# Layer 1 of a two-layer graph attention kernel: rows multiplied by ScalarE and summed by one operation a batch, V halves made a chunk ahead, groups of four tiles closed by pairs

## The reference, cut to what matters

```python
# x: (8192, 256), adj: (8192, 8192) int32, symmetric, about 8 neighbours a row and itself
h = maximum(layernorm(x), 0)                       # layer 0
x = x + leaky_relu(softmax(where(adj == 0, -1e9, e_left[:, None] + e_right[None, :])) @ (h @ W), 0.2)
h = maximum(layernorm(x), 0)                       # layer 1
h1 = h @ a[:256];  h2 = h @ a[256:]
e = leaky_relu(h1 + h2.T, 0.01)
x = x + softmax(where(adj > 0, e, -9e15), axis=1) @ h
```

## Time and profile before

| | us |
|---|---|
| times of three executions | 1916.23, 1925.32, 1924.2 |
| median | 1924.2 |
| the profiled execution's own time | 1914.35 |
| its span | 1912.5 |
| PE, busy | 1691.5 (88%) |
| DVE, busy | 1203.0 (63%) |
| ACT, busy | 973.4 (51%) |
| POOL, busy | 651.6 (34%) |

### The profile page before, as it was taken

The page is one execution under the profiler, slowest core; times in us unless marked ns, Lnnn a source line. Parts: engine busy times, 40 slices in busy tenths (PEclk is TensorE's granted clock), DMA queues, the critical chain, the costliest instruction groups (busy, mean ns, idle before and its releaser), DMA issues. The chain is left out here.

```text
span 1912.5 us, 37724 instructions
## 1 busy us (share of the span) xinstructions
PE 1691.5 (88%) x13955; PEld 1391.3 (73%) x13955; DVE 1203.0 (63%) x4595; ACT 973.4 (51%) x1367; POOL 651.6 (34%) x607
## 2 busy tenths in 40 slices
PE   6888999999999999999999397677888888978878
PEld 5646888888888888888888285454666667757657
DVE  7488888988888888674444377652435445435434
ACT  5987665665666556666662375432333233323322
POOL 0000000000000000026665548755656657665562
PEclk9998999999999999999999698877889889979889
DMA  8529998888988889989994534533333333433331
GB/s 287 182 76 386 342 349 325 314 311 321 354 320 326 318 310 331 355 333 378 386 379 104 130 94 134 160 80 88 101 89 83 111 89 94 117 100 99 88 92 52
DMA packets 142801, 410.60 MB, mean 215 GB/s; under 512 B 26193, under 2 KB 90066, under 8 KB 109906
## 3 DMA queue, kind: packets, MB, share of 16 engines
q1 hardware_dynamic: 108434, 329.85, 47.6%
q0 software_dynamic: 27904, 73.43, 13.9%
q10 hardware_dynamic: 6336, 5.77, 1.0%
HBM read 368.94 MB, written 40.03 MB: 214 GB/s over the span
## 5 line engine op out<-in xcount | busy, mean ns | idle before, releaser
L984 PE MATMUL banks<-HV,adjT 128*128 128x257 f16 x8192 | 938.8, 274 | 16.7 <-DVE adjT L658 8.8
L984 PEld LDWEIGHTS banks<-HV,adjT 128*128 128x128 fp8e4 x8192 | 792.5, 98 | 148.2 <-DVE HV L688 23.7
L1639 PE MATMUL banks<-Vp,adjp 128*128 128x257 f16 x2560 | 540.6, 292 | 115.4 <-issue 59.2
L1639 PE MATMUL banks<-Vn,adjn 128*128 128x257 f16 x2560 | 538.1, 291 | 48.9 <-issue 47.7
L1264 POOL DMA_INDIRECT gat<-h_of_layer,rec x420 | 465.8, 1109 | 275.5 <-issue 117.9
L444 ACT ACTIVATE adj_f<-adj_i 128x2048 fp8e4<-128x2048 int32 x256 | 480.1, 1898 | 6.6 <-DMA adj_i<-in_adj 6.5
L1300 ACT ACTIVATE adjn<-h1bc,nh 128x512 fp8e5<-128x512 f32 x320 | 212.1, 716 | 446.2 <-remote 272.1
L1639 PEld LDWEIGHTS banks<-Vp,adjp 128*128 128x128 fp8e4 x2560 | 261.2, 103 | 192.3 <-issue 126.5
L1639 PEld LDWEIGHTS banks<-Vn,adjn 128*128 128x128 fp8e4 x2560 | 262.2, 103 | 124.8 <-issue 76.5
L425 POOL DMA_DIRECT2D HV<-x_after_layer x44 | 25.5, 580 | 773.4 <-DVE rank L911 741.3
L1473 DVE TENSOR_TENSOR adjn<-adjp,adjn 128x1024 uint16<-128x1024 uint16 x80 | 55.4, 692 | 334.8 <-ACT adjn L1300 296.0
(11 more groups left out here) (158 smaller groups left out, 1395.2 us busy)
## 6 DMA issues: line engine op xcount, KB each, us to landing
adj_i<-in_adj SPq DMA_DIRECT2D x256, 1024.0 KB
h_of_layer<-hh SPq DMA_DIRECT2D x64, 129.0 KB
hs<-h_of_layer SPq DMA_DIRECT2D x64, 129.0 KB
xt<-in_x SPq DMA_DIRECT2D x64, 128.0 KB
packed_adj<-pk SPq DMA_DIRECT2D x64, 128.0 KB
x_after_layer<-x SPq DMA_DIRECT2D x64, 128.0 KB
HV<-in_x SPq DMA_DIRECT2D x14, 512.0 KB, 8.8
gat<-h_of_layer,rec POOLq DMA_INDIRECT x420
```

The source lines that it names most:

```text
L984: last = nc.tensor.matmul(acc[b][:, 0:DV], adjT_h[:, b, i, q, :, h], V0[:, jb, s, 0:DV], start=(jb == 0 and s == 0), stop=(jb == T - 1 and ...
L1639: mm = nc.tensor.matmul(bank[2 * i + part][:, 0:DV], m[:, i * P:(i + 1) * P], V[:, j, s, 0:DV], start=(j == 0 and s == 0), stop=(j == T - ...
```

## The change

It has four parts, all in layer 1.

1. **Rows.** ACT multiplies each gathered row by its weight in place (`scale_rows`, one instruction a row), and DVE adds up a batch by one reduction (`sum_rows`). The sum of a batch that isn't a tile's last is written behind the rows of the next batch's buffer, which has a seventh place for it, and is summed with them. Join and second accumulator are gone.
2. **When.** The weights of a batch are made in the turn of its chunk n, the larger is taken and the rows are multiplied in turn n+1, and they are summed in turn n+2. A table `taken(n)` gives the batches of chunk n: it begins with chunk 0 and holds 94 rows by the end of group 0; batches 86 and 87 (9 rows) are done behind the last chunk.
3. **V halves.** `high_chunk` and `low_chunk` make the halves a chunk or two ahead: chunk 0 ahead of everything, and then those of chunk n+2 on ACT and of chunk n+1 on DVE in turn n. `unpack` also stands one turn earlier.
4. **Closing.** In the last chunk of a group and in the first of the next one PE goes through the tiles by pairs: all four `jb` for tiles 0 and 1, and then for tiles 2 and 3. `take_sums` and `scale_sums` come in two halves, the first of which waits for the new semaphore `closed`.

```diff
-        FIRST = 1.35
-        HEAD = 3.0
+        FIRST = 1.13
+        HEAD = -2.0
+        TAIL = 1.4
...
-            gat = sb("gat", [P, NBUF, BS, ROW], f32)
-            sacc = sb("sacc", [P, 2, 2, DV], f32)
+            gat = sb("gat", [P, NBUF, BS + 1, ROW], f32)
+            sacc = sb("sacc", [P, 2, DV], f32)
...
-                        pool.wait_ge(row_added, begin[k - NBUF + 1])
+                        pool.wait_ge(summed, k - NBUF + 1)
...
+                def scale_rows(k):
+                    m, s0, s1 = batch[k]
+                    if s0 == 0:
+                        load_rows(m)
+                    act.wait_ge(w8_ready, k + 1)
+                    for i in range(s1 - s0):
+                        x = gat[:, k % NBUF, i, 0:DV]
+                        made = nc.scalar.activation(x, x, ACT.Copy, scale=w8[:, k % 2, i:i + 1])
+                    made.then_inc(scaled, 1)
...
+                high_chunk(0)
                 act.wait_ge(nh2_ready, 1)
                 act.wait_ge(h1bc_in[0], 16)
-                act.wait_ge(hb_ready, 2)
                 for h in range(2):
                     signs(h, 0, 0, 0, h, False)
+                high_chunk(1)
+                act.wait_ge(hb_ready, 2)
                 for n in range(C):
...
                     if g > 0 and c == 0:
-                        scale_sums(g - 1, g == 1)
+                        for half in range(2):
+                            scale_sums(g - 1, half, g == 1)
                     if n + 1 < C:
...
                             signs(2 * n + 2 + h, n + 1, g1 % 2, c1, h, 2 * n + 2 + h >= RB)
+                    for k in taken(n - 1):
+                        scale_rows(k)
+                    if n + 2 < NC:
+                        high_chunk(n + 2)
+                    for k in taken(n):
+                        weights(k)
+                for k in taken(C - 1):
+                    scale_rows(k)
+                for half in range(2):
+                    scale_sums(NGD - 1, half, NGD == 1)
+                for k in range(weighed[C], len(batch)):
+                    weights(k)
+                    scale_rows(k)
...
+                def sum_rows(k):
+                    m, s0, s1 = batch[k]
+                    b = s1 - s0
+                    dve.wait_ge(scaled, k + 1)
+                    if s0:
+                        dve.wait_ge(summed, k)
+                    if k == last[m]:
+                        if m >= 2:
+                            dve.wait_ge(so_ready, m - 1)
+                        to = sacc[:, m % 2, :]
+                    else:
+                        to = gat[:, (k + 1) % NBUF, batch[k + 1][2] - batch[k + 1][1], 0:DV]
+                    nc.vector.reduce_sum(to, gat[:, k % NBUF, 0:b + (1 if s0 else 0), 0:DV]
+                                         .rearrange("p s c -> p c s"), AX.X).then_inc(summed, 1)
...
+                unpack(0, 0, 0, False)
+                low_chunk(0)
                 dve.wait_ge(ab_ready, 1)
+                closing = []
                 for n in range(C):
                     g, c = n // NC, n % NC
                     negatives(n, g, c)
                     positives(n, c)
                     if g > 0 and c == 0:
-                        take_sums(g - 1)
+                        take_sums(g - 1, 0)
+                        take_sums(g - 1, 1)
+                    for m in closing:
+                        divide(m)
+                    if n + 1 < NC:
+                        low_chunk(n + 1)
+                    for m in closing:
+                        add_x1(m)
+                    closing = []
+                    for k in taken(n - 2):
+                        sum_rows(k)
+                        closing += [m for m in range(NS) if last[m] == k]
+                    if n + 1 < C and (n + 1) % UB == 0:
+                        unpack(n + 1, (n + 1) // NC, (n + 1) % NC, n + 1 >= 2 * UB)
                     if g > 0 and c == 1:
                         add_negatives(g - 1)
+                    for k in taken(n - 1):
+                        larger(k)
...
                 def group(g, first):
                     for c in range(NC):
                         n = g * NC + c
                         pe.wait_ge(pos_ready, n + 1)
                         pe.sem_inc(masks_seen, 1)
+                        halved = c == NC - 1 or (c == 0 and not first)
+                        for half in range(2 if halved else 1):
+                            some = range(half * G // 2, half * G // 2 + G // 2) if halved else range(G)
+                            for jb in range(CB):
+                                add_tile(g, c, jb, some, first)
```

More of the change, by code:

```diff
@@ L1047, in two_layer_graph_attention @@
                 batch.append((m, slots[m] * i // parts, slots[m] * (i + 1) // parts))
-        row = [(m, s, k) for k, (m, s0, s1) in enumerate(batch) for s in range(s0, s1)]
-        begin = [row.index((m, s0, k)) for k, (m, s0, s1) in enumerate(batch)]
         at = [sum(slots[:m]) for m in range(NS + 1)]
@@ L1053, in two_layer_graph_attention, with taken @@
         pace = [max(0.0, FIRST * min(n, NC) + max(0, n - NC) - HEAD) for n in range(C)]
-        rows_by = [len(row) * a / pace[-1] for a in pace]
-        rows_by = [0] + [int(a + 1e-6) for a in rows_by]
-        def lead_of(q):
-            return sum(1 for b in begin if b < q + LEAD) if q < len(row) else len(batch)
-        def ended(q):
-            if q == len(row):
-                return NS
-            return sum(1 for m in range(NS - 1) if q > at[m + 1] + min(4, slots[m + 1] - 1))
-        def awaited(q):
-            return max(0, sum(1 for m in range(NS) if at[m] < q) - 2)
+        rows_in = [at[NS] * a / (pace[-1] + TAIL) for a in pace]
+        weighed = [0] + [sum(1 for m, s0, s1 in batch if at[m] + s1 <= a) for a in rows_in]
+        def taken(n):
+            return range(weighed[n], weighed[n + 1]) if n >= 0 else range(0)
         ctx = ExitStack()
@@ L1372, in dense @@
                             if c == 0 and tail:
-                                scale_sums(g - 1, False)
+                                for half in range(2):
+                                    scale_sums(g - 1, half, False)
                     even = NGD + 1 + (NGD + 1) % 2
@@ L1380, in _ @@
                             dense(k * 2 + b, b, k * 16 + 16, True)
-                    scale_sums(NG - 1, False)
+                    for half in range(2):
+                        scale_sums(NG - 1, half, False)
             @block.vector
@@ L1592, in _ @@
-                add_negatives(NGD - 1)
+                    for k in taken(n - 1):
+                        larger(k)
+                for m in closing:
+                    divide(m)
+                    add_x1(m)
+                for k in taken(C - 2):
+                    sum_rows(k)
+                    for m in range(NS):
+                        if last[m] == k:
+                            divide(m)
+                            add_x1(m)
+                for k in taken(C - 1):
+                    larger(k)
+                    sum_rows(k)
+                    for m in range(NS):
+                        if last[m] == k:
+                            divide(m)
+                            add_x1(m)
@@ L1593, in _ @@
+                take_sums(NGD - 1, 0)
+                take_sums(NGD - 1, 1)
+                add_negatives(NGD - 1)
+                for k in range(weighed[C], len(batch)):
+                    larger(k)
+                    sum_rows(k)
+                    for m in range(NS):
+                        if last[m] == k:
+                            divide(m)
+                            add_x1(m)
                 with dve.If(dve.value_load(redi[0:1, 0:1]) > 0):
@@ L1608, in _ @@
                         dense(g, True)
-                    take_sums(NG - 1)
+                    take_sums(NG - 1, 0)
+                    take_sums(NG - 1, 1)
                     add_negatives(NG - 1)
@@ L1615, in _, with add_tile @@
                 nc.tensor.transpose(bank[7][0:T, 0:P], h1all[:, :], idf[:, :]).then_inc(h1T_ps, 1)
+                add_last = [None]
+                def add_tile(g, c, jb, some, first):
+                    j = c * CB + jb
+                    if first:
+                        pe.wait_ge(v_ready, 2 * j + 2)
+                    masks = (adjp_h[:, c // UB % 2, (c % UB * CB + jb) // 2, :, jb % 2],
+                             adjn_h[:, c % 2, jb // 2, :, jb % 2])
+                    for i in some:
+                        for part, (m, V) in enumerate(zip(masks, (Vp, Vn))):
+                            if j == 0:
+                                if first and i == 0 and part == 0:
+                                    pe.wait_ge(h1T_sb, 1)
+                                if not first:
+                                    pe.wait_ge(evn_ready if part else pos_taken,
+                                               g * G - G + i + 1)
+                                    pe.sem_inc(masks_seen, 1)
```

(5 more changed lines are left out.)

151 lines of the change are left out of this document (40 added, 111 removed).

## The result

The changed kernel takes 1993.2 us (median of four, 1978.1 to 2016.8) against 1924.8 of the kernel before; the ratio is 1.033 with a 95% interval of 1.027 to 1.039. The forecast was 1880 and a range up to 1930. The profiled execution took 1978.1, its span is 1976.2. Ratios leave out executions in a slow state of the chip, here that of 2016.8 us and further down one of 4294 us (r7), which is why 1.033 is not 1993.2 / 1924.8.

What follows compares the result with a forecast made beforehand. The prediction took PE to bound the kernel, with 254 us lost to waits and slow issue. Its terms gave 1914.4 - 19 - 18 - 10 - 6 + 13 = 1874, plus 6 for the profiled execution: 1880 us, range 1825 to 1930.

Steps and rivals of the forecast that it cites:

- What bounds the kernel: Layer 1: PE bounds; 21 stretches of slow issue, 120 us in excess, each starting 9 us or more into a POOL run.
- The other 96.5 us I leave: Groups 1 to 4: PE's remaining stalls stay as they are, 96.5 us, since POOL's work a turn is the same.
- the -18 for group 1: Group 1: its stall of 23.5 us goes, so the group takes 153 us instead of 171.
- Rows on ACT: Later turns: ACT's rows (2.0 us) and DVE's batch sums (2.7 us each) stay hidden under PE's 7.1 us.
- the slower rival: DVE's batch sums: the stride costs far more, 16 ns per output, 4.2 us a batch and more; 1938 us at 5.6; chance 0.13.
- the cheap rival: DVE's batch sums: the reduction costs 1.2 ns an element whatever the stride, giving 1856 us; chance 0.12.
- Group 0: Group 0: a chain of 10.5 us a turn, ending at 1252 against 1271, a gain of 19 us.
- Closing by pairs: Group closings: PE's waits of 14.1 us shrink, -10 us, and half the slow clock behind them goes, -6 us.
- The end: Behind the last chunk: batches 86 and 87 stand behind ACT's last sums, 28.8 us against 15.9, +13 us.
- Buffers held too long: Gather buffers: freed two turns after the gather, so PE goes at POOL's pace in parts, +45 us, 1925 us; chance 0.17.
- Stalls vanish: Groups 1 to 4: no POOL run reaches 9 us, most of the 96.5 us goes, about 1800 us; chance 0.13.

Runs made afterwards that it cites:

- r7: A follow-up run that the text does not identify further; one execution of 4294 us, in a slow state of the chip, was left out of its ratio.
- e1: Changed kernel, with POOL waiting behind each batch of gathers until the batch has landed: 1891.8 us, ratio 0.985 to the kernel before.
- e2: Kernel before, with only POOL's wait behind each batch of gathers added: 1936.3 us, ratio 1.009.
- b2: Changed kernel with a 128x1536 memset on POOL behind each batch, in a session with slow issue: 1824.8 us against 1911.3, ratio 0.951.
- c1: Changed kernel with the unpacking back at the head of its turn, in a quiet session: 1735.8 us against 1753.6 of the kernel before, ratio 0.990.
- e3: Kernel before with the closing by pairs alone: 1914.9 us, ratio 0.999.
- e4: Changed kernel with five gather buffers instead of four: 1965.2 us, ratio 1.024 to the kernel before.
- a1: Changed kernel itself, timed again in a later session beside the kernel before: 1969.0 us against 1920.9, ratio 1.024.
- r8: Changed kernel with a 128x1536 memset on POOL behind each batch, in a quiet session: 1819.2 us, ratio 1.037 to the kernel before.

## Why the prediction was wrong, by its steps

**What bounds the kernel.** Right: PE, and the 21 stretches belong to POOL's runs. e1, e2 and b2 show what was only read there. One reading was off: slow issue begins from 8.2 us into a run on, as in the run of the earlier trace rows at 1388.9, and not at 9 or more.

**The step that failed** is "The other 96.5 us I leave, as POOL's work a turn (5 x 1.37) is the same", with the -18 for group 1 beside it. POOL's work was the same, and slow issue went from 121 to 183 us. I had priced the stalls by POOL's amount of work. The runs show that they hang on gathers that follow one another without a break (e1, e2, b2), and that the new order pays more for a microsecond of such a run (0.83 to 1.02 us against 0.45 to 0.52), for a reason that stays open. Group 1 took 181.6 instead of 153, groups 2 to 4 167.3, 166.7 and 184.0 instead of some 150: together about 100 us, nearly the whole distance between 1874 and 1976.

**Rows on ACT.** Right. Five multiplied rows take 2.11 us, 0.40 apart. The reductions, by shape:

```profile
L1540 DVE TENSOR_REDUCE sacc<-gat 128x257 f32<-128x1542 f32 x20 | 59.6, 2980 | 9.8 <-ACT gat L1321 8.2 <-issue 1.5
...
L1540 DVE TENSOR_REDUCE gat<-gat 128x257 f32<-128x1028 f32 x16 | 31.3, 1954 | 0.0
...
L1540 DVE TENSOR_REDUCE gat<-gat 128x257 f32<-128x771 f32 x5 | 5.1, 1029 | 0.0
```

The mean over 88 is 226.9 / 88 = 2.58 us where 2.7 was taken. This closes both rivals on its price: 1.9 ns an element from four rows up, neither 1.2 ns an element nor 4.8 us a sum. A sum takes 10 ns per output (2.58 us / 257), where the slower rival put 16; no run shows that figure. The Trainium skill, VectorE: DVE Perf Modes, section "The perf-mode tier table", which has `tensor_reduce` at 1x whatever the type, gave the cheap rival; these rows, at 1.9 ns, decide against it for this layout. The Trainium skill, SBUF — State Buffer, section "Door 1: The DMA port swizzle", with its penalty for each new 16-byte line, agrees in direction; a stride of a row costs no more an element than the 176 bytes of the earlier trace rows.

**Group 0.** Predicted 1252, measured 1254.6, partly by luck. The turn was meant to be 10.5 us; where nothing disturbs it, ACT's rows start 8.7 us apart (1147.62, 1156.33). Waits of PE for masks (22.5 us in nine) and slow issue that I had not put down, 12.1 us in the first run of 24 gathers and 6.2 in one of 15, filled the rest. In a quiet session the group takes 144.6 us (c1, which differs by the place of the unpacking).

```profile
1147.62 2.11 ACT L1321 ACTIVATE gat<-gat,w 128x257 f32<-128x257 f32 x5 [2.08 <-DVE w L1523]
...
1156.33 2.11 ACT L1321 ACTIVATE gat<-gat,w 128x257 f32<-128x257 f32 x5 [0.55 <-DVE w L1523]
```

**Closing by pairs.** Direction right, size wrong: waits of 6.2 us remain, the longest 3.5, and e3 finds no gain that can be measured where 16 us were put down. That what PE gains at a closing is lost again in the next slow stretch would fit (slow issue is 131 us in e3, 121 before), but it isn't shown.

**The end.** Right: 22.1 us from PE's end to the span's, 22 predicted.

**Rivals.** Buffers held too long: false (e4). Stalls vanish: its mechanism, short runs, is what e1 makes by force, but the change did not make it. The slower rival had the nearest number, 1938, but named the reduction's stride, and that was the wrong mechanism. A rival was missing: that slow issue may also grow. The last sentence of the prediction names a new stall wherever POOL's runs now fall, and gives it neither a price nor a chance.

## What to carry to other kernels

When an engine slips with nothing that it waits for, look at what the other engines do without a pause at that time, and try a break there before trusting that the loss stays as it is. A long unbroken row of indirect transfers on POOL is such a thing: with one memset per batch the changed kernel went from 2.4% behind the kernel before to 5% ahead of it (a1, b2). In a quiet session the same memset left it 3.7% behind (r8), so such a break is worth its price only where slow issue is about. Time the kernel before in the same session, since here it alone moved by 9% between sessions.

## What the runs showed of the hardware

Where slow issue is about, it begins in the changed kernel mostly 7 to 10 us into an unbroken run of gathers, after some seven of them, in the kernel before 8 to 24 us into it (once 113), and it mostly ends 1 to 3 us behind the run's end; PE then issues an instruction about every 0.7 us; 1032 or 256 bytes a row make no difference; a break of 1.56 us with a memset in it (b2) or of 2.1 us with POOL idle (e1) takes most of it away. In quiet sessions a run of 249 us (c1) does nothing. What path the two engines share, and what makes a session quiet, no run here shows.

A reduction of rows read with the stride of a row costs 1.9 to 2.0 ns an element from 1028 elements up but 1.33 at 771 (three rows), a step that no run here explains.
